# First expert stage: products to SBUF on VectorE, their low parts on GpSimd

## What is computed

```python
combine = jnp.zeros((T, NUM_EXPERTS)).at[jnp.arange(T)[:, None], top_idx].set(top_w)
h1 = jax.nn.silu(jnp.einsum('th,eih->eti', x, w_gate))
h1w = h1 * combine.T[:, :, None]
routed = jnp.einsum('eti,ehi->th', h1w, w_down)
```

## Time and profile before

| | |
|---|---|
| three runs | 1056.14, 1063.99 and 1060.61 us, median 1060.61 |
| span of the profiled execution | 1054.7 us |
| TensorE busy | 1006.9 us, 95% of the span |
| VectorE busy | 808.3 us, 77% |
| ScalarE busy | 804.5 us, 76% |
| GpSimd busy | 235.8 us, 22% |

### The profile page before, as it was taken

How to read it: one execution, slowest core, us unless ns; L and a number is a source line. 1 busy time by engine, 2 the same in 40 slices (tenths; PEclk the granted TensorE clock), 3 DMA queues, 4 the chain that set the end, 5 groups by cost and what they waited for, 6 DMA issues and landing times.

```text
span 1054.7 us, 20344 instructions
## 1 busy us (share of the span) xinstructions
PE 1006.9 (95%) x5274; PEld 681.7 (65%) x5274; DVE 808.3 (77%) x1837; ACT 804.5 (76%) x1356; POOL 235.8 (22%) x371
## 2 busy tenths in 40 slices
PE   5799999999997999999999999999998998999997
PEld 3333333333335688888888888888884887788885
DVE  8644444444448799999999999999995788699997
ACT  5799999999996787887887877878875553855554
POOL 3776765554463000000000000000005112300000
PEclk9799999999999999999999999999999999999999
DMA  4477876777651587767777777777731000034331
GB/s 134 144 230 238 256 253 219 230 231 229 223 202 40 178 310 248 238 235 240 238 245 240 245 233 239 245 241 245 245 107 60 1 2 1 1 128 125 115 95 40
DMA packets 102991, 188.98 MB, mean 179 GB/s; under 512 B 11932, under 2 KB 56604, under 8 KB 102940
## 3 DMA queue, kind: packets, MB, share of 16 engines
q1 hardware_dynamic: 102756, 188.19, 55.0%
q10 hardware_dynamic: 192, 0.30, 0.1%
HBM read 152.46 MB, written 35.98 MB: 179 GB/s over the span
## 4 chain that ended last, share of the span: by engine, by line
PE 86%; DVE 4%; ACT 4%; DMA 2%; POOL 1%; issue 1%; SPq 0%; DVEq 0%; ACTq 0%; POOLq 0%
PE bank L1483 28%; PE bank L1496 16%; PE bank L1381 12%; PE bank L1490 8%; PE bank L1365 6%; PE bank L1362 6%; PE bank L1581 1%; PE bank L1392 1%; PE bank L1204 1%; DVE state L2056 1%; POOL rstd L690 1%; PE bank L1591 1%; DVE stats L1705 1%; ACT xn L882 1%; PE bank L1586 1%
## 5 line engine op out<-in xcount | busy, mean ns | idle before, releaser
L1483 PE MATMUL bank<-xh,w_parts 128*128 128x512 f32 x896 | 276.6, 390 | 2.2 <-ACT xn L1131 1.3
L983 ACT ACTIVATE ring<-bank,minus_bound 128x1024 f32<-128x1024 f32 x256 | 263.0, 1118 | 13.9 <-PE bank L1365 9.0
L1082 ACT ACTIVATE bank<-bank 128x512 f32<-128x512 f32 x320 | 186.2, 582 | 88.8 <-PE bank L1483 88.8
L1970 DVE TENSOR_TENSOR bank<-bank,ring 128x512 f32<-128x512 f32 x320 | 223.9, 700 | 25.3 <-DMA ring<-c_rows 2.4
L1496 PE MATMUL bank<-hh,w_parts 128*128 128x512 f32 x772 | 238.1, 390 | 0.0
L1962 DVE TENSOR_TENSOR hl<-bank,hh 128x512 fp32r<-128x512 f32 x321 | 218.5, 681 | 0.1
L1862 DVE TENSOR_TENSOR bank<-bank,corner 128x128 f32<-128x128 f32 x256 | 76.4, 299 | 154.9 <-PE bank L1365 153.8
L1483 PEld LDWEIGHTS bank<-xh,w_parts 128*128 128x128 f32 x896 | 167.3, 188 | 39.0 <-DVEq L1956 1.7
L1076 ACT ACTIVATE hh<-bank 128x512 fp32r<-128x512 f32 x321 | 190.4, 593 | 1.0 <-DVE bank L1970 0.9
L1483 PE MATMUL bank<-xl,w_parts 128*128 128x512 f32 x448 | 174.4, 389 | 0.0
L1496 PEld LDWEIGHTS bank<-hh,w_parts 128*128 128x128 f32 x772 | 144.9, 188 | 30.5 <-ACT hh L1076 0.8
(11 more groups left out here) (324 smaller groups left out, 1137.8 us busy)
## 6 DMA issues: line engine op xcount, KB each, us to landing
ring<-c_rows SPq DMA_DIRECT2D x173, 512.0 KB, 4.7
w_parts<-w_pairs SPq DMA_DIRECT2D x160, 128.0 KB, 2.9
w_pairs<-xh SPq DMA_DIRECT2D x16, 768.0 KB, 4.4
q_stack<-q_parts SPq DMA_DIRECT2D x63, 144.0 KB
k_stack<-k_parts SPq DMA_DIRECT2D x189, 48.0 KB
w_pairs<-xl SPq DMA_DIRECT2D x16, 512.0 KB, 2.9
big<-in_w_exp SPq DMA_DIRECT2D x16, 384.0 KB, 4.9
w_ffn_parts<-xl SPq DMA_DIRECT2D x16, 384.0 KB, 3.8
```

The lines of the kernel that those rows point to most:

```text
L983: act.activation(ring[:, c % RING * S:(c % RING + 1) * S], wide[(m + c) % SB][:], ACT.Exp, bias=minus_bound[:]).then_inc(exp_done, 1)
L1082: act.activation(bank(4 + c % ZB), bank(4 + c % ZB), ACT.Silu).then_inc(silu_ready, 1)
L1483: ins = pe.matmul(out_, w[i], x_[j], start=start and k == 0, stop=stop and k == 2, skip_group_check=not start)
L1970: dve.tensor_tensor(bank(4 + c % ZB), bank(4 + c % ZB), cb[u][:, g * GW:(g + 1) * GW], ALU.mult).then_inc(hid_ready, 1)
```

## The change

VectorE writes its products to four SBUF tiles (`weighted`, which is `shared_z`) and no longer in place in PSUM. ScalarE makes the high parts from there. The low parts are subtracted by GpSimd, in a loop of its own that stands before its wait for the stage's end. ScalarE's high part of item n-1 now also waits for the low part of item n-3, and VectorE's product of item n for the low part of item n-4. The tile of zeros that opens the pipeline is now an SBUF tile, and VectorE's wait ahead of it is for its own earlier work (`shared_ready`) and not for the first combine weights (`cb_loaded[0]`).

```diff
+        weighted = shared_z
@@ GpSimd
+            def low_part(n, c):
+
+                ready(pool, hh_ready, n - 1)
+                pool.wait_ge(low_used, n + (1 + CREDIT))
+                pool.tensor_tensor(hl[(c - 1) % 2][:], weighted[(c - 1) % 4], hh[(c - 1) % 2][:].bitcast(F32), ALU.subtract).then_inc(hl_ready, 1)
+
+            with pool.Fori(0, MT_N // CB) as i:
+                for c in range(CB * G):
+                    low_part(i * (CB * G) + c, c)
+            low_part(MT_N * G, 0)
             pool.wait_ge(acc_done, 1)
@@ ScalarE
-                    high_part(n, c, bank(4 + (c - 1) % ZB), hid_ready, down_done, hh_ready)
-            high_part(MT_N * G, 0, bank(4 + ZB - 1), hid_ready, down_done, hh_ready)
+                    act.wait_ge(hl_ready, n + CREDIT)
+                    high_part(n, c, weighted[(c - 1) % 4], hid_ready, down_done, hh_ready)
+            act.wait_ge(hl_ready, MT_N * G + CREDIT)
+            high_part(MT_N * G, 0, weighted[3], hid_ready, down_done, hh_ready)
@@ VectorE
-            dve.wait_ge(cb_loaded[0], 16)
-            dve.memset(bank(4 + ZB - 1), 0.0).then_inc(hid_ready, CREDIT)
+            dve.wait_ge(shared_ready, G)
+            dve.memset(weighted[3], 0.0).then_inc(hid_ready, CREDIT)
@@
-                    dve.tensor_tensor(bank(4 + c % ZB), bank(4 + c % ZB), cb[u][:, g * GW:(g + 1) * GW], ALU.mult).then_inc(hid_ready, 1)
-                    low_part(n, c, bank(4 + (c - 1) % ZB), hh_ready, low_used, hl_ready)
-            low_part(MT_N * G, 0, bank(4 + ZB - 1), hh_ready, low_used, hl_ready)
+                    dve.wait_ge(hl_ready, n + (CREDIT - 1))
+                    dve.tensor_tensor(weighted[c % 4], bank(4 + c % ZB), cb[u][:, g * GW:(g + 1) * GW], ALU.mult).then_inc(hid_ready, 1)
```

## The result

The changed kernel takes 1082.62 us (median of 4 runs, 1081.64 to 1085.86) against 1058.38 before (median of 4, 1053.61 to 1063.99). The ratio is 1.0244, with a 95% interval of 1.0214 to 1.0275: slower. The profiled span went from 1054.7 to 1080.8, 26.1 us more; by the medians it is 24.2.

A forecast was written before the change was run, and what follows sets the result against it. The prediction took TensorE as the bound in the expert stage; 0.1 us at the start plus 18 us of late hand-overs, on 1060.6, gave 1078.6, say 1078 us, with 8 in 10 for 1059 to 1096.

The forecast's parts named there:

- The bound: Expert stage: TensorE bounds, busy all 430.17 us; VectorE, busy 407, is close, but relieving it frees nothing anyone waits for.
- The rate of GpSimd: Low part on GpSimd: 1.28 us fits under the 1.361 us step, 0.08 to spare, so no bound.
- rival 2: GpSimd's low part takes 1.51 us beside VectorE: steps of 1.494 us, 42 us more, 1103; chance 0.07.
- The latency: Hand-over of the low part to `down_low`: 0.17 us late, 0.057 us a step over 316 steps, 18 us.
- the hop: From the high part's end on ScalarE to the low part's start on GpSimd: taken as 0.14 us, between 0.08 and 0.24.
- From t: t is the start of step n+1's first matmul; `down_low` of item n was due at t+3.40, forecast at t+3.57.
- The start: Stage opening: product 0 still starts when its combine weights land, at 357.61; nothing gained, 0.1 us lost.
- The end: Last low part ends at 794.2, its `down_low` starts at 796.55 behind the shared expert's sums; hidden by 2 us.
- (1): Hand-over to `down_low`: the low part is in time, steps stay 1.361 us, 1060.6 us; chance 0.22.
- (3): GpSimd's loop: 0.21 us of issue behind each low part, 1.49 us a step, some 41 us up, 1102; chance 0.05.
- (4): Faster by relief of VectorE or PSUM, at about 1048 us; chance 0.03.

The follow-up runs named there:

- the last two of the experiments: Kernel before with silus in SBUF: low part reading the silu there, 1056.64 us; also VectorE's product written to SBUF unread, both parts from the silu, 1056.09 us.

## Why the prediction was right

The forecast was 1078 us, slower, by a late hand-over to `down_low`; it came to 1082.6. The mechanism held. The size was low: 18 us of loss were forecast, and it is 24.2 by the medians and 26.1 by the spans. That the time itself is only 4.6 us off is in part luck, since the sum started from 1060.6, the median of three runs, and with a fourth run the kernel before stands at 1058.4. Three terms of the sum were small, and one wasn't there.

**The bound.** Right: VectorE's relief (busy half the time now) frees nothing, as TensorE was never waiting for it.

**The rate of GpSimd.** Right that it is no bound. I had 1.28 us from L864; it is 1.293 to 1.294, and even at 1.296 the kernel with the later `down_low` has no wait for it. The company of VectorE's products costs it 0.015 us at most (rival 2 asked for 0.23).

**The latency.** The mechanism is shown from both ends: 0.08 us off the hop gives 0.08 / 3 a step (8.7 us), and with that same hop a step of slack takes the rest away (14.4 us), together 1.4459 to 1.3729 a step, 23 us, for the 18 of the sum. From t the sum was 1.99 + 0.14 + 1.28 + 0.05 + 0.79 = 4.25 us for three steps; the trace has 1.99 + 0.16 + 1.30 + 0.05 + 0.80 = 4.30 in the window shown. The hop is the first of the terms that were small, 0.16 for 0.14, and the low part the second. The hop's 0.16 comes, as the prediction had it, from the wait on the register row. What stands ahead of the prediction says that VectorE's low part had both waits on the instruction; in the trace its `low_used` has a row of its own, met ahead, and the subtraction carries the wait for the high part. Over the whole stage three steps take 4.34. The other 0.04, the third small term, goes with matmuls of 392 to 395 ns; how much of it the matmuls are is not split further.

**A term that wasn't there.** That a read of SBUF by ScalarE makes TensorE's matmuls longer no row of before told. Alone it is worth 0.012 to 0.020 us a step, 4 to 6 us. In the changed kernel it lies partly under the wait for GpSimd, so the two don't simply add. By steps: 0.073 for the lateness and 0.012 for what stays with the slack, 0.085 x 316 = 26.7 us; less the 0.9 by which silu 3 was earlier that is 25.8, and the span grew by 26.1. Why 0.012 stays with low parts on GpSimd and 0.019 with low parts on VectorE isn't shown.

**The start.** Predicted 0.1 lost, measured 0.9 won, but the change isn't shown to have won it. The sum took product 0 to start at 357.61, when its combine weights land; it started 0.80 us earlier:

```profile
356.81 1.29 DVE L1985 TENSOR_TENSOR k_stack<-bank,ring 128x512 f32<-128x512 f32 x2 [5.89 <-DMA ring<-c_rows]
```

The transfer that it waits for was issued 0.81 us earlier too (352.12 and 352.93), so the gain comes from ahead of it. Three kernels that open the stage as the kernel before does, the one with the silu in SBUF and the last two of the experiments, have silu 3 at 358.86 to 359.67 as well. From product 0 to silu 3 it is 2.95 us, and was 3.04: the opening itself is as long as it was.

**The end.** As predicted: the last low part ends at 820.45 and its `down_low` starts at 822.89, behind the shared expert's sums, so it only moves with the rest.

**The rivals.** (1) The low part in time: falls, 256 waits for it; it takes four `hl` buffers for two and a later `down_low`, and then 0.3% is still lost. (2) A longer instruction in company: not with one input in PSUM; with two in SBUF it comes, and larger than I had priced it (1165 us, not 1103). (3) Issue not hidden: falls, since low parts in the kernel with the later `down_low` follow one another at 0.06 to 0.12 us, and each is released by its high part. (4) Faster: falls.

No kernel tried is faster than the one before beyond its interval. Even free of the lateness, the change moves work off an engine that nobody waits for.

## What to carry to other kernels

In a software pipeline ask two questions of a slower engine: does its instruction fit into a step, and does it end before the step that takes its result. Here 1.30 of 1.36 us fits, and it was still 0.2 us late; lateness divided by the number of steps in the loop, times the steps of the stage, gave most of the loss, and one more step of slack in the buffers took it away. In the trace, look also at which row carries the late wait: here that made half of the hop, and the source doesn't tell it, since the changed kernel and the one with the later `down_low` write the two waits in the same order and get different rows. And an engine that is 95% busy without anyone waiting for it (VectorE before, 407 of 430 us) isn't worth relieving: look for the waits, not for the load.

## What the runs showed of the hardware

- From the end of ScalarE's instruction to the start of GpSimd's that waits for it: 0.08 us where GpSimd's instruction carries that wait itself (one wait only: 248 of 248; with a second wait met ahead on a row of its own: 255 of 255), 0.14 where the late wait stands on a semaphore row ahead of it (228 of 228) and 0.16 where it stands on the register row (243 of 243), the instruction then carrying the long met one.
- A 128x512 f32 subtraction on GpSimd takes 1.29 us, 1.9 times VectorE's 0.68.
- GpSimd with two SBUF inputs beside VectorE with two SBUF inputs: 1.74 us for 1.30, and 1.56 to 1.77 for 0.69 to 0.70. With one of VectorE's in PSUM neither shows more than 0.02.
- ScalarE reading its 128x512 input from SBUF in place of PSUM (624 ns for 594) lengthens TensorE's matmuls beside it from 389 ns to 391 to 393, and a step from 1.361 to 1.382 us.
